# The first two blocks of context and key weights in a tile of their own: two full-row transfers, and the even blocks scaled on VectorE

## The reference

```python
features_n = rmsnorm(features, fn_w)                      # ctx_4096: 4 x 64 tokens, 1024 wide
K = jnp.einsum('bsd,fd->bsf', features_n, Wk_w) + Wk_b
Q = jnp.einsum('btd,fd->btf', text, Wq_w) + Wq_b          # text: layernorm(x), 4 x 512 tokens
scores = jnp.einsum('btf,bsf->bts', rmsnorm(Q, qn_w), rmsnorm(K, kn_w)) / sqrt(1024)
attended = jnp.einsum('bts,bsf->btf', softmax(scores), features_n)
x = x + tanh(g_xattn) * attended
x = x + tanh(g_ffn) * ffn(layernorm(x))                   # base matmul + gated experts
```

## Time and profile before

| | |
|---|---|
| time, median of 3 runs | 470.49 us (470.21 to 470.55) |
| the profiled execution's own time | 470.91 us |
| its span, first to last instruction | 469.1 us |
| mean granted clock of TensorE | 1.000 |
| TensorE busy in matmuls | 464.3 us of the span, 99% |
| VectorE, ScalarE, GpSimd busy | 360.1, 172.6, 119.6 us |
| transfers | 84.40 MB, mean 180 GB/s |

### The profile page before, as it was taken

How to read it: one execution, slowest core, us unless ns; L and a number is a source line. 1 busy time by engine, 2 the same in 40 slices (tenths; PEclk the granted TensorE clock), 3 DMA queues, 4 the chain that set the end, 5 groups by cost and what they waited for, 6 DMA issues and landing times.

```text
span 469.1 us, 6945 instructions
## 1 busy us (share of the span) xinstructions
PE 464.3 (99%) x2481; PEld 398.3 (85%) x2481; DVE 360.1 (77%) x750; ACT 172.6 (37%) x349; POOL 119.6 (26%) x107
## 2 busy tenths in 40 slices
PE   8999999999999999999999999999999999999997
PEld 7898999998888888888888887888888888888886
DVE  1777996868889968779988887967758678875833
ACT  4947541341224214226335426332241521413400
POOL 0021511003344353336253306031040502205000
PEclk9999999999999999999999999999999999999999
DMA  8995129857577378577379640220504131050202
GB/s 308 410 411 228 80 91 376 341 180 294 191 254 248 134 247 293 198 283 240 149 265 421 286 143 37 73 109 13 169 0 136 45 109 71 2 179 1 90 1 90
DMA packets 22114, 84.40 MB, mean 180 GB/s; under 512 B 2624, under 2 KB 3904, under 8 KB 19264
## 3 DMA queue, kind: packets, MB, share of 16 engines
q1 hardware_dynamic: 21792, 83.81, 49.1%
q10 hardware_dynamic: 288, 0.15, 0.1%
HBM read 61.93 MB, written 22.02 MB: 179 GB/s over the span
## 4 chain that ended last, share of the span: by engine, by line
PE 91%; DMA 6%; DVE 2%; issue 0%; ACT 0%; DVEq 0%; SPq 0%
PE bank L664 11%; PE bank L784 9%; PE bank L788 9%; PE bank L786 9%; PE bank L700 7%; PE bank L702 7%; PE bank L701 7%; PE bank L757 4%; PE bank L545 4%; DMA bt_raw<-bt_dram 3%; DMA out_dram<-xs 2%; PE bank L686 2%; PE bank L685 2%; PE bank L687 2%; PE bank L736 2%; PE bank L737 2%
## 5 line engine op out<-in xcount | busy, mean ns | idle before, releaser
L1575 POOL TENSOR_TENSOR small<-small,tiny 128x1 f32<-128x1 f32 (+2 forms) x25 | 23.6, 942 | 167.7 <-DVE small L1201 140.6
L1555 DVE SCALAR_TENSOR_TENSOR xs<-bank,tiny,xs 128x512 f32<-128x512 f32 (+1 forms) x61 | 43.1, 739 | 24.1 <-PE bank L788 18.5
L700 PE MATMUL bank<-xth,gram 128*128 128x512 f32 x144 | 57.3, 398 | 0.0
L702 PE MATMUL bank<-xtl,gram 128*128 128x512 f32 x144 | 56.2, 390 | 0.0
L701 PE MATMUL bank<-xth,gram 128*128 128x512 f32 x144 | 56.1, 390 | 0.0
L1603 POOL TENSOR_TENSOR sq_sum<-sq_sum,sq 128x512 f32<-128x512 f32 x24 | 32.0, 1332 | 57.1 <-DVE sq L1383 57.1
L784 PE MATMUL bank<-wh_T,zh 128*128 128x512 f32 (+1 forms) x116 | 46.1, 397 | 0.4 <-DVE xs L1555 0.4
L784 PE MATMUL bank<-wh_B,zh 128*128 128x512 f32 x116 | 46.3, 399 | 0.0
L788 PE MATMUL bank<-wh_B,zl 128*128 128x512 f32 x116 | 45.3, 391 | 0.0
L786 PE MATMUL bank<-wl_B,zh 128*128 128x512 f32 x116 | 45.2, 390 | 0.0
L788 PE MATMUL bank<-wh_T,zl 128*128 128x512 f32 (+1 forms) x116 | 44.6, 384 | 0.0
(11 more groups left out here) (200 smaller groups left out, 1129.1 us busy)
## 6 DMA issues: line engine op xcount, KB each, us to landing
xst<-x_dram SPq DMA_DIRECT2D x16, 512.0 KB, 4.2
xz<-xt_dram SPq DMA_DIRECT2D x16, 512.0 KB, 7.9
out_dram<-xs SPq DMA_DIRECT2D x14, 512.0 KB, 2.7
xa<-x_dram SPq DMA_DIRECT2D x12, 512.0 KB, 4.2
x<-xa SPq DMA_DIRECT2D x12, 512.0 KB, 3.1
xs<-x SPq DMA_DIRECT2D x12, 512.0 KB, 4.0
wq_raw<-wq_dram SPq DMA_DIRECT2D x8, 512.0 KB, 14.0
t_raw_T<-wb_dram SPq DMA_DIRECT2D x4, 1024.0 KB, 16.1
```

The lines of the kernel that those rows point to most:

```text
L700: pe.matmul(acc[:, :], gram[:, g, 0, :], xth[b % 2][:, r, :], start=r == ROWS[j][0], stop=False)
L702: done = pe.matmul(acc[:, :], gram[:, g, 0, :], xtl[b % 2][:, r, :], start=False, stop=r == ROWS[j][-1])
L1555: dve.scalar_tensor_tensor(out=xs[slot][:, cols], in0=bank[n_bank][:, 0:hi - lo], scalar=tg[:, 1:2], in1=xs[slot][:, cols], op0=ALU.mult, ...
```

## The change

- A new tile `lead_sb`, in space that is unused at this stage, holds `fw`, context block 0, weight block 0, context block 1 and weight block 1, side by side in each partition. The host lays out an input `lead` in the same way. Two transfers fill it: the first has `fw` and both blocks 0 (2080 bytes in each partition), the second both blocks 1 (2048 bytes). Each is one run per partition on both sides. The transfer of line 827 with c = 0 is gone; those with c = 1, 2, 3 stay as they were. SyncE waits for the second of the new ones where it waited for c = 0.
- VectorE scales the even blocks and ScalarE the odd ones. Block 0 waits for the first new transfer, block 1 for both. `k01` takes weight blocks 0 and 1 from `lead_sb`.
- `vecs` loses `fw` (16 KB instead of 20). It is issued behind ScalarE's one-column copy instead of ahead of it, and is waited for in `small` and `key_bias` instead of in the first `ct`.
- The cleared tile and the wait for it are gone: warm-up matmuls and the one-column copy read a constant of the program, broadcast. The warm-up is three matmuls of 256 columns and one of 128, instead of five of 256.

```diff
+        lead_sb = at("lead_sb", [P, FB + 4 * S_ALL], F32, r_pt)
+        fw = lead_sb[:, 0:FB]
+        LEAD = [slice(0, FB + 2 * S_ALL), slice(FB + 2 * S_ALL, FB + 4 * S_ALL)]
+        ct_lead, wk_lead = ([lead_sb[:, FB + n * S_ALL:FB + (n + 1) * S_ALL] for n in ns] for ns in ((0, 2), (1, 3)))
-        vecs = own("vecs", [P, 5, FB])
+        vecs = own("vecs", [P, 4, FB])
-        idle = at("idle", [P, 2 * P + 2], F32, r_z)
+        idle = at("idle", [P, 1], F32, r_z)
+        zeros = nc.const_aps.tensor(0.0, [P, 2 * P])
-        IDLE = 5
+        IDLE = (2 * P, 2 * P, 2 * P, P)
...
-            pe.wait_ge(v_idle, 1)
-            for n in range(IDLE):
-                pe.matmul(bank[T_BANKS[0]][:, 0:2 * P], idle[:, 0:P], idle[:, 0:2 * P], start=True, stop=True)
+            for width in IDLE:
+                pe.matmul(bank[T_BANKS[0]][:, 0:width], zeros[:, 0:P], zeros[:, 0:width], start=True, stop=True)
...
-                        pe.wait_ge((a_ct, v_ct)[c % 2], c // 2 + 1)
+                        pe.wait_ge((v_ct, a_ct)[c % 2], c // 2 + 1)
+                        block = wk01[:, c, :, :] if c > 1 else wk_lead[c].rearrange("p (f m) -> p f m", f=2)
...
-            for c in range(4):
+            for n in range(2):
+                sp.dma_start(lead_sb[:, LEAD[n]], lead[:, LEAD[n]]).then_inc(ld_lead[n], 16)
+            for c in range(1, 4):
                 sp.dma_start(ct_wk01[:, :, c, :], front[:, c, :, :]).then_inc(ld_ct[c], 16)
-            sp.wait_ge(ld_ct[0], 16)
+            sp.wait_ge(ld_lead[1], 16)
...
+            act.activation(idle[:, :], zeros[:, 0:1], ACT.Copy)
             act.dma_start(vecs[:, :, :], vec).then_inc(ld_vec, 16)
-            act.wait_ge(v_idle, 1)
-            act.activation(idle[:, 2 * P:2 * P + 1], idle[:, 2 * P + 1:2 * P + 2], ACT.Copy)
...
-                    act.wait_ge(ld_ct[c], 16)
+                    k = 2 * c + 1
                     if c == 0:
-                        act.wait_ge(ld_vec, 16)
-                    k = 2 * c
-                    act.activation(ct[:, k, :], ct[:, k, :], ACT.Copy, scale=fw[:, k:k + 1]).then_inc(a_ct, 1)
+                        act.wait_ge(ld_lead[0], 16)
+                        act.wait_ge(ld_lead[1], 16)
+                    else:
+                        act.wait_ge(ld_ct[c], 16)
+                    act.activation(ct[:, k, :], ct[:, k, :] if c > 0 else ct_lead[1], ACT.Copy, scale=fw[:, k:k + 1]).then_inc(a_ct, 1)
...
                 elif stage == "key_bias":
+                    act.wait_ge(ld_vec, 16)
...
-            dve.memset(idle[:, :], 0.0).then_inc(v_idle, 1)
-
...
-                    dve.wait_ge(ld_ct[c], 16)
+                    k = 2 * c
                     if c == 0:
-                        dve.wait_ge(ld_vec, 16)
-                    k = 2 * c + 1
-                    dve.tensor_scalar(ct[:, k, :], ct[:, k, :], fw[:, k:k + 1], None, ALU.mult).then_inc(v_ct, 1)
+                        dve.wait_ge(ld_lead[0], 16)
+                    else:
+                        dve.wait_ge(ld_ct[c], 16)
+                    dve.tensor_scalar(ct[:, k, :], ct[:, k, :] if c > 0 else ct_lead[0], fw[:, k:k + 1], None, ALU.mult).then_inc(v_ct, 1)
...
                 elif stage == "small":
+                    dve.wait_ge(ld_vec, 16)
```

More of the change, by code:

```diff
@@ L41, in empty, with build @@
         return engine, sum(e == engine for e in self.emptied_by[:n + 1])
-def build(nc, x, xt, ctx, front, wq, wk, wb, hd, bt, vec, fn_w, b_base, scal, out):
+def build(nc, x, xt, ctx, lead, front, wq, wk, wb, hd, bt, vec, fn_w, b_base, scal, out):
     T, D = x.shape
@@ L134, in build @@
         wk01 = ct_wk01[:, 1, :, :].rearrange("p c (k f m) -> p (c k) f m", k=CK, f=2)
+        lead_sb = at("lead_sb", [P, FB + 4 * S_ALL], F32, r_pt)
+        assert (r_px, r_pe) == (r_pt + ROW // 2, r_pt + ROW)
+        fw = lead_sb[:, 0:FB]
+        LEAD = [slice(0, FB + 2 * S_ALL), slice(FB + 2 * S_ALL, FB + 4 * S_ALL)]
+        ct_lead, wk_lead = ([lead_sb[:, FB + n * S_ALL:FB + (n + 1) * S_ALL] for n in ns] for ns in ((0, 2), (1, 3)))
         wkf = [at(f"wkf{f}", [P, KB, P], F32, o) for f, o in enumerate(r_wk)]
@@ L221, in build @@
         assert r_p3 + (TPB + 2) * P * WORD <= r_g + SLOT
-        bq, bk, qn, kn, fw = (vecs[:, i, :] for i in range(5))
+        bq, bk, qn, kn = (vecs[:, i, :] for i in range(4))
         ctx_ss, ctx_tmp, ctx_rs = (small[:, k:k + 2] for k in (0, 2, 4))
@@ L261, in build @@
         ld_vec, ld_sc, ld_fnw, ld_bt, ld_bb = (sem(f"ld_{n}") for n in ("vec", "sc", "fnw", "bt", "bb"))
-        ld_ct = [sem(f"ld_ct{i}") for i in range(4)]
+        ld_lead = [sem(f"ld_lead{i}") for i in range(2)]
+        ld_ct = [None] + [sem(f"ld_ct{i}") for i in range(1, 4)]
         ld_xt = [sem(f"ld_xt{i}") for i in range(4)]
@@ L277, in build @@
             sem(f"p_{n}") for n in ("ring", "k", "g", "m", "mr", "y", "s", "hd", "prod", "fin"))
-        v_idle = sem("v_idle")
         p_first, a_first, v_first = (sem(f"{n}_first") for n in "pav")
@@ L611, in tensor @@
                     for c in range(KB):
-                        pe.wait_ge((a_ct, v_ct)[c % 2], c // 2 + 1)
+                        pe.wait_ge((v_ct, a_ct)[c % 2], c // 2 + 1)
+                        block = wk01[:, c, :, :] if c > 1 else wk_lead[c].rearrange("p (f m) -> p f m", f=2)
                         for f in range(2):
-                            done = pe.matmul(k_at(f), wk01[:, c, f, :], ct[:, c, :], start=f == c == 0, stop=c == KB - 1,
+                            done = pe.matmul(k_at(f), block[:, f, :], ct[:, c, :], start=f == c == 0, stop=c == KB - 1,
                                              skip_group_check=True)
@@ L1664 @@
     columns = [np.asarray(v).reshape(D // P, P).T
-               for v in (L0_xattn_Wq_b, L0_xattn_Wk_b, L0_xattn_qn_w, L0_xattn_kn_w, L0_xattn_fn_w)]
+               for v in (L0_xattn_Wq_b, L0_xattn_Wk_b, L0_xattn_qn_w, L0_xattn_kn_w)]
     B, T, S = x.shape[0], x.shape[1], ctx_4096.shape[0] * ctx_4096.shape[1]
+    front = np.stack(
+        [ctx_4096.reshape(S, D // P, P).transpose(2, 1, 0).reshape(P, 4, -1),
+         np.asarray(L0_xattn_Wk_w)[0:2 * P].reshape(2, P, D // P, P).transpose(3, 2, 0, 1).reshape(P, 4, -1)], axis=2)
     arrays = {
@@ L1670 @@
         "ctx": np.ascontiguousarray(ctx_4096.reshape(-1, D)),
-        "front": np.ascontiguousarray(np.stack(
-            [ctx_4096.reshape(S, D // P, P).transpose(2, 1, 0).reshape(P, 4, -1),
-             np.asarray(L0_xattn_Wk_w)[0:2 * P].reshape(2, P, D // P, P).transpose(3, 2, 0, 1).reshape(P, 4, -1)], axis=2)),
+        "lead": np.ascontiguousarray(np.concatenate([np.asarray(L0_xattn_fn_w).reshape(D // P, P).T,
+                                                     front[:, 0, :, 0:S].reshape(P, -1), front[:, 0, :, S:].reshape(P, -1)], axis=1)),
+        "front": np.ascontiguousarray(front),
         "wq": np.ascontiguousarray(np.asarray(L0_xattn_Wq_w).reshape(-1, P, D)),
```

## The result

The changed kernel takes **472.75 us** (median of 6 runs, 471.91 to 473.86) against 470.48 us (6 runs, 470.19 to 471.04). The ratio is 1.0048, 95% interval 1.0034 to 1.0061: 0.5% slower, outside the predicted 469.8 to 471.1. The profiled execution took 472.10 us with a span of 470.3; that of before took 470.91 with 469.1. In two of the six runs, 473.61 and 473.86, the mean granted clock of TensorE was 0.996, in the others 1.000. The median of those four is 472.31, 1.83 above before.

What follows compares the result with a forecast made beforehand. TensorE, busy 464.3 of 469.1 us, bounds the kernel, but a full transfer queue holds it at Wq's sixth slab. The 0.56 us gain is swallowed there: span 469.1 + 0.0, profiled 470.91, median 0.42 lower, so 470.5 us; range 469.8 to 471.1.

Steps and rivals of the forecast that it cites:

- The bound, the place and the chain: From first packet to Wq's sixth slab, a full transfer queue, ScalarE and VectorE set the time; TensorE has no part.
- slab 5: Sixth slab of Wq, where TensorE meets its data: wait grows from 0.30 to 0.86 us, left at 41.99 as before.
- TensorE's wait at block 2: In k01, block 2 is ready only at 6.63, so TensorE waits 0.28 us.
- swallowed as forecast: TensorE's 0.56 us earlier arrival is lost waiting at Wq's sixth slab, so the sum is 0; chance 0.70.
- c = 1 stays at 6.23: At the stream's start, the transfer behind the two new ones lands when it did before, 6.23.
- the extra transfer costs the stream: Rival at the stream's start: an unoverlapped fixed 2.8 us makes wq4 late, 473.3 (472.5 with 2.0 us); chance 0.03.
- The first landing: First 260 KB land at 4.20, 0.68 us ahead of 4.88, so k01 starts at 4.60; 4.88 the other bound.
- The clock: Rival in k01: a gap of 0.4 to 0.9 us delays the clock's rise, 0.48 us slower, 470.97; chance 0.08.
- the warm-up: Ahead of k01, the shortened matmuls take 3.0 us and end at 3.7 to 4.2.
- `vecs`: Issued behind ScalarE's copy at 2.69, landed at 6.0, needed at 9.35; rival that it is late, chance 0.03.
- Slack at `wqh0`: At Wq's start, TensorE 0.56 us earlier wants wqh0 at 15.16; it is ready at 13.83.

Runs made afterwards that it cites:

- 2: Kernel before with only the two new transfers added, warm-up, engines and issue of vecs as before: 472.31 us, ratio 1.0031.
- 8: Kernel before with its first 512 KB transfer cut in two of 256 KB, out of front into the same tile: 472.38 us, ratio 1.0043.
- 1: Changed kernel with blocks 0 and 1 brought by the one transfer of before and fw in vecs: 471.79 us, ratio 1.0012.
- 7: Changed kernel with the new tensor brought by one transfer of 516 KB instead of two: 470.74 us, ratio 1.0001.
- 15: Changed kernel with the second new transfer issued from ScalarE's queue, so SyncE issues c = 1 at 1.17: 470.69 us, ratio 1.0004.
- 3: Changed kernel with fw in a slot of 64 words, so each run starts at a multiple of 256 bytes: 471.90 us, ratio 1.0032.
- 4: Changed kernel with c = 1 to 3 each as one 4 KB run per partition, tile laid out to match: 472.29 us, ratio 1.0023.
- 9: Changed kernel with SyncE waiting for c = 1 instead of the second new transfer before later loads: 473.28 us, ratio 1.0044.
- 10: Changed kernel without SyncE's wait, later loads issued right behind c = 3: 472.05 us, ratio 1.0031.
- 11: Changed kernel with ScalarE and VectorE waiting for c = 1 before they scale blocks 0 and 1: 475.87 us, ratio 1.0101.
- 12: Changed kernel with vecs issued only behind ScalarE's work on block 3: 473.35 us, ratio 1.0045.
- 17: One-transfer form of 7 with SyncE waiting for GpSimd's constants, so c = 1 is issued at 1.60 instead of 1.17: 472.26 us, ratio 1.0038.
- 18: Kernel before with c = 1 waiting for ScalarE's one-column copy, so issued at 2.72, 1.5 us later: 471.78 us, ratio 1.0028.
- 14: Changed kernel with c = 1 to 3 as one transfer of 1.5 MB, blocks 2 to 7 waiting for all of it: 476.42 us, ratio 1.0115.
- 16: Kernel before with no edit, profiled once more in one execution: 470.96 us.
- 5: Changed kernel with front laid out transfer by transfer in memory: 471.08 us, ratio 1.0011.
- 6: Kernel before with front laid out transfer by transfer in memory: 471.16 us, ratio 1.0016.
- 13: Changed kernel with one 516 KB new transfer and front laid out transfer by transfer: 471.53 us, ratio 1.0018.

## Why the prediction was wrong

**The bound, the place and the chain: right for the changed kernel, but not the only way.** There the chain from the stream over wq4, ScalarE and VectorE ended last at slab 5: wq4 came 1.88 us later, slab 5 was left 1.89 later. The four runs at full clock are 1.83 slower in the median; that this is so near 1.89 is partly luck, since the profiled one won 0.61 back at `xs`. The stream had a second way to the time that the prediction had at 0.28 us, TensorE's wait at block 2. It measured 2.4 us and alone would have made slab 5 some 1.05 us late; in 2 and 8 it is the whole of the lateness there. The early start gave nothing, but not by being swallowed as forecast: TensorE came to slab 4 1.42 us late, not 0.56 early.

**"c = 1 stays at 6.23": the step that failed.** I took the pace of four transfers of 512 KB, issued some 0.5 us apart, for a rate that any division of the bytes keeps. That transfer landed at 8.01, 1.78 us later. The two transfers alone do it (2), a plain cut of c = 0 does it (8), and without two short ones on one queue it is gone (1) or mild (7, 15: 324 and 332 GB/s, and no loss of time). Excluded by runs as what makes it: alignment (3), rows in two runs (4), SyncE's wait and the loads behind it (9, 10), the engines' reads (11), `vecs` (12).

**The rival "the extra transfer costs the stream": right in its place, near in its price, wrong in its reason.** It gave 473.3, and 472.5 by the figure of the Trainium skill, which the page ("DMA: Bandwidth & Descriptors", Anatomy of one DMA) states for transfers issued from GpSimd, as these are not. I gave it 0.03. The mechanism was a fixed cost for each transfer that doesn't overlap. Experiment 15 has as many transfers in all as the change and 1.0004; experiment 17 has as few as before and 1.0038. So it isn't the count as such. What 17 and 18 show is that the moment of issue can cost as much. In the change it is later too: the first 512 KB are 516 KB in two issues, and c = 1 is issued at 1.65, not at about 1.2 (0.73 and a quarter of the 2.00 us of the earlier trace rows; 1.17 in experiment 7). A delay there, by itself, costs 0.4% (0.43 us, 7 against 17) and 0.3% (1.5 us, 18). That it is the cause in the change is not shown: no run has the two short transfers on one queue and c = 1 issued at 1.17, or on two queues and c = 1 at 1.65. What I argued against the rival, the even 1.353 us between the four of `front`, was evidence for transfers with a full one ahead of them at the queue, and I used it for one with 256 KB ahead.

The Trainium skill ("DMA: Bandwidth & Descriptors", Bandwidth) advises transfers of 1 MiB or more. These runs bear it out only in that two of 260 and 256 KB did worse than one of 516 KB (1.0048 against 1.0001). One of 1.5 MB behind them landed no earlier than three of 512 KB (10.53 against 10.63, 14). And the kernel before runs at 407 GB/s with 512 KB each, so what hurts here is not the size as such.

**The first landing.** Predicted 4.20, with 4.88 the other bound; measured 3.55. I had scaled only the data part; the rest shrank as well, from 2.8 us to 2.82 - 0.68 = 2.1. A part of that may be spread, for the first landing of the kernel before was 4.88 in one execution and 4.67 in the other (16). The list of transfers, 0 to 16 us (KB each, median us from issue to landing):

```profile
lead_sb<-lead_dram SPq DMA_DIRECT2D x1, 260.0 KB, 2.8
lead_sb<-lead_dram SPq DMA_DIRECT2D x1, 256.0 KB, 3.1
vecs<-vec_dram ACTq DMA_DIRECT2D x1, 16.0 KB, 2.9
```

`k01` therefore began at 3.96, not at 4.60, and the wait at block 2 was 2.4 us where I had 0.28: 8.42 against 6.63. TensorE handed over to `k` 1.26 us later than before, not 0.56 earlier.

**The clock.** My rival had it rise late because of the gap ahead of `k01`. That didn't happen: the warm-up ends at 3.95, as forecast within 3.7 to 4.2, and runs into `k01` without a break; the eight instructions from 3.96 take 2.10 us. It can happen for all that: in the traces of 3, 5 and 9, with the same start, the eight take 3.47, 3.08 and 3.23 us, at steps of 0.43 for all or most of them. It cost nothing there, as c = 1 came later still. But the gap at block 2 is a new one, and two of six runs have a mean clock of 0.996 and are 1.4 us above the median of the other four. Experiments 11 and 14 show what longer gaps do. That the 2.4 us gap does it in some runs is likely, and not shown: no profiled run of the changed kernel fell among them.

**`vecs`.** Predicted issue at 2.69 and landing at 6.0, measured 0.80 and 3.7 (0.80 + 2.9): the issue didn't wait for the copy ahead of it to be done (2.04 + 0.20). It was in time, as said, and first used at 10.90, when c = 3 was through. **Slack at `wqh0`:** no wait there, as said.

**What stays open.** The runs show that issuing c = 1 late costs; that in the change it is late against its turn, because half as much data goes ahead of it, fits but accounts for only part. Experiment 17, with c = 1 issued as late and one transfer ahead, has 278 GB/s and a mild stretch, the change 196. Nor does a late issue by itself say why packets take longer for each byte, 1.45 times in the change and 1.30 times in 17, where the transfer engines are hardly ever without one. Why the stretch lasts until 6.4 us, long after the later issues are in the queue, why the layout in memory bears on it (5), why the kernel before loses its even pace with the other layout (6), and why 5 and 7 together are worse than 7 (13), no run here tells.

No version tried beats the kernel before. One transfer for both blocks (7) and two queues (15) come out equal to it: both start `k01` at 4.5, 0.9 us earlier, and leave slab 5 at 42.19 and 42.16, against 41.99: there the gain is swallowed, as the prediction had it for the change.

## What to carry to other kernels

When a transfer at the head of a full stream is made shorter, ask first what it does to those behind it: each issue takes its 0.4 to 0.5 us, and a short transfer gives the next one less time to be issued in. An even spacing in the trace holds for the issue times and sizes that made it, not for others. And where a later meeting point is bound by the stream, an earlier start is worth nothing while a late stream can cost at two places, at its first use and at that meeting point, and the later of the two sets the time; a rival of that shape deserves more than 0.03.

## What the runs showed of the hardware

- The rate of the transfers fell to 195 and 196 GB/s, half of 407, for 2.8 us behind transfers of 260 and 256 KB on one queue (2 and the change), and only to 332 when the second of them came from ScalarE's queue (15). Of the fall in the change, the transfer engines were without a packet for part (share 0.74 for 1.06), and packets took 1.45 times as long per byte for the rest.
- Issuing the three transfers behind the first 0.43 us later, with 516 KB under way, cost 0.4% of the kernel (7 against 17).
- ScalarE's queue issued `vecs` at 0.80 while the engine was loading its function table (0.74 to 2.02) and its one-column copy had not begun (2.04).
- TensorE ran at 0.50 of its clock for some three microseconds after a gap of 4.96 us (14). After one of 4.54 us the steps show the same (11), though the granted clock reads 1.00 there.
